# Score maxima and score copies read in pairs of tiles

## The reference

```
Q, K, V = x Wq + bq, x Wk + bk, x Wv + bv            # per batch b and head h: (1024, 8)
for w in 0..15:
    m      = cos(phase_modulators[w, h])
    s      = (Q m)(K m)^T / sqrt(8);  s = s cos(KERR s s)
    acc   += softmax(s) V * interference_weights[w]
x = layernorm(x + (acc / 16) Wo + bo)
x = layernorm(x + mixture_of_experts(x))             # 8 experts of 128 x 512, top 2 of 9 gates
```

## Time and profile before

| | |
|---|---|
| time, median of 3 runs | 6975.69 us (6973.81 to 6976.5) |
| profiled execution, its own time | 6975.18 us |
| its span in the profile | 6973.7 us |
| TensorE matmuls busy | 6097.9 us (87%) |
| VectorE busy | 6061.4 us (87%) |
| ScalarE busy | 6796.0 us (97%) |
| score reductions, line 823 | 512, 599.7 us busy |
| score copies, line 833 | 512, 601.3 us busy |
| granted TensorE clock, mean | 0.957 of full |

### The profile page before, as it was taken

One profiled execution on the slowest core, in us unless ns is written; L12 is line 12 of the kernel. 1 busy time (PEld: TensorE's weight loads), 2 busy tenths in 40 slices (PEclk: granted clock), 3 DMA queues, 4 the chain that ended last, 5 costly groups with the idle time before them and its releaser, 6 DMA issues.

```text
span 6973.7 us, 125248 instructions
## 1 busy us (share of the span) xinstructions
PE 6097.9 (87%) x47364; PEld 2296.8 (33%) x47364; DVE 6061.4 (87%) x8039; ACT 6796.0 (97%) x1209; POOL 148.7 (2%) x244
## 2 busy tenths in 40 slices
PE   7888888888889888889888898888888888988888
PEld 3222222222333333333333333333333333333336
DVE  7998899899888888898888888888988888888884
ACT  6999999999999999999999999999999999999993
POOL 0000000000000000000000000000000000000000
PEclk8999999999999999999999999999999999999999
DMA  2000000000101001000010010010010100100100
GB/s 60 3 5 5 5 3 5 5 3 5 33 22 30 18 28 30 17 28 27 22 30 23 22 30 18 28 30 17 28 30 20 30 25 20 30 18 28 30 16 35
DMA packets 60481, 150.52 MB, mean 22 GB/s; under 512 B 11168, under 2 KB 27424, under 8 KB 59680
## 3 DMA queue, kind: packets, MB, share of 16 engines
q1 hardware_dynamic: 52960, 136.89, 6.3%
q0 software_dynamic: 2816, 3.68, 0.8%
q10 hardware_dynamic: 4160, 2.10, 0.1%
HBM read 132.14 MB, written 10.49 MB: 20 GB/s over the span
## 4 chain that ended last, share of the span: by engine, by line
ACT 48%; PE 35%; issue 13%; ACTq 4%; DVE 1%; DMA 0%; SPq 0%; DVEq 0%
ACT ring L593 46%; PE pv L705 23%; ACTq L590 3%; PE sc L753 3%; PE pv L711 3%; PE tr L721 2%; PE sc L765 2%; ACT tile_h L632 1%; PE sc L1337 1%; PE tr L1347 1%; PE sc L672 1%; PE sc L653 0%; ACT L632 0%; ACTq L591 0%; PE sc L290 0%
## 5 line engine op out<-in xcount | busy, mean ns | idle before, releaser
L593 ACT ACTIVATE ring<-scores 128x7168 f32<-128x7168 f32 (+1 forms) x1023 | 6581.5, 6529 | 7.3 <-PE pv L711 3.6
L705 PE MATMUL pv<-ring,vh 128*32 128x512 f32 x30400 | 3944.4, 627 | 821.8 <-ACT ring L593 812.8
L705 PEld LDWEIGHTS pv<-ring,vh 128*32 128x32 f32 x30400 | 992.8, 114 | 3422.5 <-issue 2081.5
L862 DVE SCALAR_TENSOR_TENSOR vprobs<-ring,vprobs 128x1024 f32<-128x1024 f32 x592 | 725.3, 1225 | 20.4
L861 DVE SCALAR_TENSOR_TENSOR ring<-ring 128x1024 f32<-128x1024 f32 x592 | 725.2, 1225 | 20.3
L860 DVE SCALAR_TENSOR_TENSOR vprobs<-ring,vprobs 128x1024 f32<-128x1024 f32 x592 | 721.2, 1218 | 7.1
L833 DVE COPY scores<-sc 128x1024 f32<-128x1024 f32 (+1 forms) x512 | 601.3, 1216 | 111.3 <-PE sc L672 111.3
L823 DVE TENSOR_REDUCE rowmax<-sc 128x1 f32<-128x1024 f32 x512 | 599.7, 1213 | 20.0 <-PE sc L653 12.8
L711 PE MATMUL pv<-vprobs,vlast 128*32 128x512 f32 x2368 | 613.0, 592 | 3.7 <-DVE vprobs L862 2.5
L703 PE MATMUL pv<-vpower,vlast 128*32 128x512 f32 x2368 | 613.7, 594 | 0.0
L850 DVE TENSOR_SCALAR vprobs<-scores,scales_log 128x1024 int32<-128x1024 f32 (+1 forms) x592 | 440.7, 744 | 43.9 <-DVE vprobs L862 25.2
(11 more groups left out here) (161 smaller groups left out, 2572.9 us busy)
## 6 DMA issues: line engine op xcount, KB each, us to landing
tile_w<-in_L_ffn_w SPq DMA_DIRECT2D x192, 512.0 KB, 3.9
qt<-q_scratch SPq DMA_DIRECT2D x256, 36.0 KB
kt_<-k_scratch SPq DMA_DIRECT2D x256, 36.0 KB
ring<-in_L_ffn_w SPq DMA_DIRECT2D x2, 2048.0 KB, 10.5
ring<-in_L_attn_x ACTq DMA_DIRECT2D x4, 512.0 KB, 7.2
q_scratch<-ring SPq DMA_DIRECT2D x4, 512.0 KB, 3.9
k_scratch<-ring SPq DMA_DIRECT2D x4, 512.0 KB, 4.9
v_scratch<-ring SPq DMA_DIRECT2D x4, 512.0 KB, 5.0
```

What stands on the lines that cost most here:

```text
L593: nc.scalar.activation(ring[:, i % SLOTS, 0:cols], scores[:, bass.ds(n % 2, 1), :, :].rearrange("p o k s -> p (o k s)")[:, 0:cols], ACT.Ex ...
L705: last = nc.tensor.matmul(sums, vh[:, buf, kt, window], ring[:, w % SLOTS, kt * S + qh * HALF:kt * S + (qh + 1) * HALF], start=(first and ...
L862: nc.vector.scalar_tensor_tensor(probs, vmant, EXP2_BETA, probs, ALU.add, ALU.mult).then_inc(vexp_step, 1)
```

## The change

VectorE reads both places of `sc` in one instruction. `reduce_max(m, t)` now waits for tiles t and t + 1, reduces 128 x 2 x 1024 to two columns of `rowmax`, and counts `sc_free` up by two. `copy_scores(m, k)` does the same for tiles k and k + 1, one copy of 2048 columns. They are called half as often, everywhere. `shifted_tile` puts tile k into place k % 2 instead of (9 + k) % 2, so that the even tile of a pair is in place 0. TensorE's instructions, their order and the numbers that they wait for are the same; since `sc_free` goes up in twos, the wait of an even tile t for t - 1 reads is met when the whole pair before it has been read.

```
             nc.vector.tensor_copy(peak[:, 0:2], recip[:, 0, 0:2]).then_inc(peak_step, 1)
-            for t in range(2):
-                reduce_max(dve, 0, t)
+            reduce_max(dve, 0, 0)
...
-            for t in range(2, KT):
+            for t in range(2, KT, 2):
                 reduce_max(dve, 0, t)
             set_row(dve, 0)
-            for k in range(KT):
+            for k in range(0, KT, 2):
                 copy_scores(dve, 0, k)
...
-                last = nc.tensor.matmul(slot_of(use)[:, cols], head_k[first:first + ROWS, k * P:(k + 1) * P],
+                last = nc.tensor.matmul(slot_of(k)[:, cols], head_k[first:first + ROWS, k * P:(k + 1) * P],
...
         def reduce_max(dve, m, t):
-            dve.wait_ge(sc_full, USES * m + t + 1)
-            nc.vector.tensor_reduce(rowmax[:, t:t + 1], sc[:, t % 2, :], axis=AX.X, op=ALU.max).then_inc(sc_free, 1)
+            dve.wait_ge(sc_full, USES * m + t + 2)
+            nc.vector.tensor_reduce(rowmax[:, t:t + 2], sc[:, :, :], axis=AX.X, op=ALU.max).then_inc(sc_free, 2)
...
         def copy_scores(dve, m, k):
-            use = ROW_USE + 1 + k
-            dve.wait_ge(sc_full, USES * m + use + 1)
-            nc.vector.tensor_copy(scores[:, bass.ds(m % 2, 1), k, :].rearrange("p o s -> p (o s)"), sc[:, use % 2, :]).then_inc(sc_free, 1)
+            dve.wait_ge(sc_full, USES * m + ROW_USE + 1 + k + 2)
+            nc.vector.tensor_copy(scores[:, bass.ds(m % 2, 1), k:k + 2, :].rearrange("p o k s -> p (o k) s"), sc[:, :, :]).then_inc(sc_free, 2)
...
                     if at < 4:
                         reduce_max(dve, n + 1, 2 * at)
-                        reduce_max(dve, n + 1, 2 * at + 1)
...
                         copy_scores(dve, n + 1, 2 * (at - 6))
-                        copy_scores(dve, n + 1, 2 * (at - 6) + 1)
```

## The result

| | before | changed |
|---|---|---|
| time, median of 13 runs each | 6974.41 us (6972.96 to 6977.19) | 6989.87 us (6986.85 to 6991.67) |
| profiled execution, its span | 6975.18, 6973.7 us | 6987.75, 6986.3 us |
| start of the first full exponential | 81.42 us | 90.34 us |
| idle time before the exponentials | 7.0 us | 10.6 us |
| granted clock, mean | 0.957 | 0.958 |

The ratio is 1.0021, with an interval of 1.0012 to 1.0029: 15.5 us slower by the medians, 12.6 by the two profiled executions. The predicted 6982.7 had the sign and half of the size, and its range ended at 6986.

What follows compares the result with a forecast made beforehand. ScalarE's exponentials were taken to bound the kernel, with everything before the first full one delaying the end. First head 3.1 + 3.1 + 1.06 = 7.26 us, loop zero: 6982.7 us predicted, +0.10%, 8-in-10 range 6979 to 6986.

Steps and rivals of the forecast that it cites:

- What bounds the kernel: Whole kernel: ScalarE's exponentials bound it, 97% of the span; delays before 81.4 us move the end one for one.
- The pair read, 2.28 us: VectorE's 2048-column read: 2.28 us, bounds 2.12 and 2.43; some 38 us of VectorE saved, booked at zero.
- The first head, 7.26 us: First head: serial turns add 3.1 us in reductions, 3.1 in copies, 1.06 for a ScalarE piece; bounds 6.0 to 8.5.
- broadcast and `set_row`: First head, row maxima broadcast and added between reductions and copies: unchanged, only moved by 3.1 us.
- the last ScalarE piece: First head, first wavelength: one more ScalarE piece stands behind the last copy, +1.06 us.
- the turn: First head, pair of tiles then pair read: 2.12 + 2.28 + 0.06 = 4.46 us, 1.06 more than now.
- The loop, zero: Main loop: pairs cost zero because both ends of every pair stay where they are; lower bound -7.0 us.
- "No cost": Rival: TensorE gets the full clock in the first head; 6970 to 6977 us, point value 6975; chance 0.08.
- "Slower beyond doubt": Rival: burstier TensorE work slows waves with feed-forward matmuls in the loop, about +28 us, 7010; chance 0.04.
- A worse clock phase: Rival: the same serial turns plus 1 to 3 us from TensorE's clock, 6984 to 6986 us; chance 0.16.
- The signs listed: Timeline: 2.28 us reads, 256 of each kind, first full exponential at 88.7 us, exponentials' idle time 5 to 9 us.
- "Same": Whole kernel: measured time not told from no change, about 0.2% or 14 us; chance 0.93.

Runs made afterwards that it cites:

- e15: Kernel before with pairs only in the loop, plus sixteen one-element memsets at the head of VectorE's stream; 6972.93 against 6973.56 us, -0.6.
- e1: Kernel before with pairs only in the first head, single reads in the loop; 6983.74 against 6974.11 us, +9.6.
- e17: Changed kernel with sixteen one-element memsets at the head of VectorE's stream, timed; 6981.17 against 6973.56 us for the kernel before, +7.6.
- e2: Kernel before with pairs only in the loop, first head on single tiles; 6977.87 against 6974.11 us, +3.8.
- e4: Changed kernel again, unedited, against the kernel before; 6987.16 us, +13.0, ratio 1.0019.
- e7: Changed kernel with extra filler matmuls on TensorE behind each first-head pair of tiles and the broadcast; 6981.17 against 6973.65 us for the kernel before, +7.5.
- e9: Changed kernel with 16 no-operations at the head of VectorE's stream; 6986.09 us, +12.4 against the kernel before.
- e10: Changed kernel with 16 no-operations at the end of the body of VectorE's first loop; 6985.95 us, +12.3 against the kernel before.
- e12: Changed kernel with score matmuls over 32 rows, the added rows zeros; 6986.61 us, +13.1 against the kernel before.
- e13: Changed kernel with sixteen one-element memsets at the head of VectorE's stream, one run; 6983.61 us.
- e3: Kernel before with single reads everywhere, only shifted tile k put in place k % 2; 6973.25 us, -0.9, ratio 1.0000.
- e14: Changed kernel with fifteen one-element memsets at the end of the body of VectorE's first loop, one run; 6983.95 us.
- e16: Kernel before with filler matmuls only behind the first two score tiles (14) and the broadcast (6); 6974.00 us, +0.4, ratio 1.0001.
- e8: Kernel before with filler matmuls: 14 after the first two tiles, one after every single first-head tile, 5 after the broadcast; 6983.20 us, +9.6.
- e11: Kernel before with score matmuls over 32 rows instead of 8 and 9, the added rows zeros; 6975.96 us, +2.5.

## Why the prediction was wrong, step by step

**What bounds the kernel: right.** What is late before the first full exponential moves the end, and VectorE's length is worth nothing: its 37 us saved (583.5 + 585.6 us against 599.7 + 601.3 in the table) never came back: e15, with pairs in the loop and no stall on the path, is 0.6 us below the kernel before, within noise.

**The pair read, 2.28 us: right.** 2.279 and 2.288 us.

**The first head, 7.26 us: right in mechanism, short by 1.05 us** in the profiled execution. From the first reduction to the last one's end it took 16.08 us (49.72 to 65.80) instead of 12.57, so +3.51 where +3.1 was forecast; the copies +3.50 instead of +3.1; broadcast and `set_row` +0.34 instead of 0, at the low clock; the last ScalarE piece +0.96 instead of 1.06. Sum 8.31. The mis-sized term is the turn: 4.60, not 4.46 us. Its 2.12 us for a pair of tiles was taken from one tile; a pair takes 2.25 us until its read starts (56.66 to 58.91), six times 0.14 in all. Further 0.6 us of the 8.9 by which the first full exponential is late are there before the first reduction (49.72 against 49.11); its start lies anywhere from 47.6 to 50.3 us in the traces of all versions. By medians the first head's pairs cost 9.6 us (e1, pairs there only) and 7.6 us (e17, all pairs without the stall), on either side of the sum.

**The loop, zero: this step failed.** It was put as "So the loop's cost is zero", "because both ends of every pair stay where they are". For the pairs that is true: e15 measures -0.6 us. What the step left out is that fewer instructions also move every later instruction of VectorE. In order of code, up to the end of the first loop's body, the trace records 438 instructions of VectorE instead of 454. All seven traces with 438 (the changed kernel, e2, e4, e7, e9, e10 and e12) have the stall at the loop's end, none of the ten with 453 or 454 has it, e13 to e15 and e17 among them. With 438 the wait for the next piece of code, which before fell 50 us behind the loop's end and held up nothing, falls on that end, 2.9 us, ahead of a reduction with a chain of tiles, value products and ScalarE behind it.

ScalarE loses 2.4 to 2.5 us there in the traces of the changed kernel, e2, e4, e7 and e10 (0.66 in e9 and 0.38 in e12, with the same stall), and nothing in those of e1, e3, e13, e14, e15 and e17. The size of the gap goes with TensorE's clock: the two tiles and the value products behind the stall took 7.4 us in the five traces with the large gap, 6.5 in e9 and 6.2 in e12, where the clock was back at 1.00 for part of them. By the medians the stall costs more, 13.0 - 7.6 = 5.4 us and 3.8 - (-0.6) = 4.4 us. With intervals of 6 us to either side this excess over the visible gap isn't settled, and the traces don't support it: from the first full exponential to the end of the last one the seven traces with the stall take 6741.0 to 6745.5 us (mean 6743.7), the ten without it 6739.1 to 6742.9 (mean 6741.3), 2.4 us less.

**The bill:** the traces show 8.3 us for the first head and about 2.4 for the stall, 10.7 together; by medians it is 7.6 and 5.4, which is e4's +13.0 by construction. The 2 us between the two ways of counting stay open, and so do the 2.5 us between e4 and the 15.5 of the first comparison. The same is true of e7: a first head 0.4 us late plus the stall makes 3 us by the traces, 5.8 by medians, and 7.5 was measured.

**The rivals.** "No cost" needed a clock above 0.9 in the first head; it was 0.50, and e7, where fillers gave it 1.00, shows what the condition is worth: the first full exponential is then 0.4 us late (1.1 us, counted from the first reduction). The 3.51 us forecast for a turn at the full clock were 3.65. That it would be only 0.11 us more than now compared it with a turn at the low clock; against e16's 2.43 it is 1.22 more. "Slower beyond doubt" didn't happen: but for the one at the loop's end, no wait before an exponential is longer than 0.7 us, as before. A worse clock phase was worth little: from the first full exponential to the end of the last one the changed kernel takes 6745.53 us, before 6740.67; of the 4.9 us 2.4 are the stall, and about 2 come as 0.1 us a head in heads 1 to 15, at one wave where TensorE's low clock recurs. e1 shows the same drift without pairs in the loop, e4 none with them, and in either kernel these few microseconds come and go between traces. That it goes with the moment at which the loop starts is argued, not shown.

**The signs listed.** Pair reads and counts as forecast; the reads of the first head at 49.72, 54.32, 58.91 and 63.51 and at 72.32 to 86.11 us, up to 1.8 us later than listed; first full exponential at 90.34, inside the 86 to 91 allowed; the idle time before exponentials grew by 3.6 us, and the bound for "wrong" was 3. That sign pointed at the failed step before any experiment did: 2.4 of the 3.6 us are the one wait at the loop's end.

**The range.** It held the uncertainty of prices of what I had listed (clock, turn) and nothing for a place that the edit moves without naming it. "Same" got 0.93, with 0.2% as what can be told from no change; the interval's lower end is 0.12% and its middle 0.21%.

## What to carry to other kernels

A double buffer given up costs nothing where the reader comes late anyway, and the overlap in every turn where the stage is nothing but produce and read (here 1.2 us a turn, at either clock); find those stages first. A higher clock shortens both kinds of turn, so compare them at the same clock. Fewer instructions are also moved instructions: after any edit of a looped stream, look for "issue" waits of some microseconds behind loop ends, and compare where they fell before. If one lands on the critical path, move the code by a few cheap instructions, which here took back 2.4 us by the traces and 5.4 of 13.0 by medians.

## What the runs showed of the hardware

- VectorE can stall at or behind the end of a loop until an instruction packet has been fetched: 2.9 to 3.1 us at the loop's end in the seven traces that have it there, 2.0 to 3.1 us some 50 us later in the others but e14 (0.8 us). Fifteen or sixteen instructions more or less decide at which instruction it falls. The Trainium skill (Runtime: NRT & Kernel Launch, "Instruction fetch mechanics") says that a branch out of the part already fetched forces a fetch before execution goes on; the trace fits that for the stall at the loop's end, with a packet at 1738.91 us, 1.5 us behind the branch, and work again at 1740.64. That the target lay outside that part was not tried by itself, and the waits 50 us later stand at no loop's end.
- A turn of two score tiles took 2.43 us double-buffered and 3.65 us serial at a granted clock of 1.00 (e16, e7), 3.40 and 4.60 us at 0.50.
- TensorE's clock fell to half while the engine was busy in every microsecond of the stretch (e8: 0.63, later 0.50), and stayed full with a filler behind each pair (e7: 1.00) at 10.08 of 13.00 us.
- Making the score matmuls 32 rows high with zeros left the first head's clock low (0.60 and 0.50 in e11) and cut the low-clock stretches in the loop from 125 to 75, for no time gained.
- Sixteen no-operations on VectorE left no record in the trace; sixteen one-element memsets did, and moved the code.
